# Last chunk pair of the Walsh-Hadamard mix on VectorE, two weight column sums behind the gate stage

## What is computed

```python
def fwht(x):          # normalized Walsh-Hadamard transform over the last dim (1024)
    ...
        x = jnp.stack([a + b, a - b], axis=-2).reshape(-1, n)
def bitlinear(x, w):   return jnp.einsum('bsh,oh->bso', act_quant(x), weight_quant(w))
def h_bitlinear(x, w): return jnp.einsum('bsh,oh->bso', act_quant(fwht(x)), weight_quant(w))
gate = bitlinear(x, w_gate)
up = bitlinear(x, w_up)
intermediate = jax.nn.silu(gate) * up
return h_bitlinear(intermediate, w_down)
```

## Time and profile before

| | |
|---|---|
| runs | 398.34, 399.23, 401.84 us, median 399.23 |
| profiled execution | 401.39 us, its span 399.6 us |
| VectorE busy | 338.6 us (85%) |
| ScalarE busy | 321.7 us (80%) |
| TensorE busy | 309.2 us (77%), weight load 190.9 us (48%) |
| GpSimd busy | 144.3 us (36%) |
| mean granted clock of TensorE | 0.906 of full speed |
| gate stage, from its first matmul to the first Hadamard matmul | 74.6 to 104.8 us |
| from there to the first exponential of the second attention | 104.8 to 159.6 us |

### The profile page before, as it was taken

One profiled execution on the slowest core, in us unless ns is written; L12 is line 12 of the kernel. 1 busy time (PEld: TensorE's weight loads), 2 busy tenths in 40 slices (PEclk: granted clock), 3 DMA queues, 4 the chain that ended last, 5 costly groups with the idle time before them and its releaser, 6 DMA issues.

```text
span 399.6 us, 7596 instructions
## 1 busy us (share of the span) xinstructions
PE 309.2 (77%) x2637; PEld 190.9 (48%) x2637; DVE 338.6 (85%) x556; ACT 321.7 (80%) x523; POOL 144.3 (36%) x315
## 2 busy tenths in 40 slices
PE   6978998777797897558676766877677767789856
PEld 5755555432585885244344443444344444433424
DVE  4665898876889888887899999799999999868996
ACT  3783679974637578899999989899999999977972
POOL 5432345459700322213224555421322132338430
PEclk9996999698699899996999988799999998995687
DMA  8900003600120003768898978789789986900001
GB/s 257 395 3 1 2 7 107 256 1 2 15 90 2 1 2 53 109 129 138 163 177 157 160 135 146 132 145 178 136 160 152 156 147 123 169 2 1 26 28 53
DMA packets 120006, 41.10 MB, mean 103 GB/s; under 512 B 114720, under 2 KB 118432, under 8 KB 119200
## 3 DMA queue, kind: packets, MB, share of 16 engines
q1 hardware_dynamic: 119536, 40.03, 50.7%
q0 software_dynamic: 144, 0.52, 0.3%
q10 hardware_dynamic: 288, 0.07, 0.1%
HBM read 11.24 MB, written 1.05 MB: 31 GB/s over the span
## 4 chain that ended last, share of the span: by engine, by line
PE 26%; ACT 26%; DVE 24%; issue 16%; POOL 6%; DMA 1%; SPq 0%; ACTq 0%; DVEq 0%; POOLq 0%
ACT rb L956 17%; PE ps L1908 4%; DVE nm L1440 4%; PE ps L2003 3%; PE ps L2108 2%; PE ps L1881 2%; PE ps L2015 1%; DVE st L1096 1%; DVE ra L1545 1%; PE ps L2065 1%; DVE small L1547 1%; POOL ra L543 1%; POOL ra L544 1%; DMA xs<-x 1%; PE ps L1780 1%
## 5 line engine op out<-in xcount | busy, mean ns | idle before, releaser
L1440 DVE TENSOR_REDUCE nm<-ps 128x1 f32<-128x1024 f32 x128 | 153.4, 1217 | 15.1 <-PE ps L2003 14.2
L956 ACT ACTIVATE rb<-ps,eb,sq 128x1024 int16<-128x1024 f32 x128 | 153.9, 1219 | 7.9 <-POOL eb L625 7.4
L2003 PE MATMUL ps<-ra,rb 128*128 128x512 bf16 x256 | 83.1, 409 | 46.7 <-ACT rb L956 45.7
L625 POOL TENSOR_SCALAR eb<-nm,sq 128x1 f32<-128x1 f32 x128 | 34.2, 267 | 122.6 <-DVE nm L1440 121.6
L2003 PEld LDWEIGHTS ps<-ra,rb 128*128 128x128 bf16 x256 | 15.9, 100 | 65.6 <-ACT rb L956 62.7
L2030 PEld LDWEIGHTS ps<-ra,tern 128*128 128x128 f16 x624 | 25.3, 97 | 15.5 <-issue 3.8
L956 ACT ACTIVATION_READ_ACCUMULATOR rb<-ps,eb,sq 128x1 f32 x128 | 27.8, 217 | 0.0
L2030 PE MATMUL ps<-ra,tern 128*128 128x16 f16 x624 | 25.8, 170 | 2.0 <-DVE rb L1171 1.4
L1881 PE MATMUL ps<-xqT,tern 128*128 128x512 bf16 x64 | 19.0, 440 | 5.4 <-DVE rb L1349 4.4
L2015 PEld LDWEIGHTS ps<-idh,rb 128*128 128x128 f16 x224 | 15.0, 103 | 14.9 <-issue 8.4
L2015 PE MATMUL ps<-idh,rb 128*128 128x128 f16 x224 | 18.4, 229 | 4.5 <-issue 2.2
(11 more groups left out here) (240 smaller groups left out, 725.6 us busy)
## 6 DMA issues: line engine op xcount, KB each, us to landing
stage<-w SPq DMA_DIRECT2D x2, 1024.0 KB, 6.7
rb<-ra SPq DMA_DIRECT2D x16, 128.0 KB, 2.9
xs<-x SPq DMA_DIRECT2D x4, 256.0 KB, 4.8
cx<-ctx_in SPq DMA_DIRECT2D x4, 256.0 KB, 5.1
stage<-w_gate SPq DMA_DIRECT2D x1, 1024.0 KB, 7.9
stage<-w_up SPq DMA_DIRECT2D x1, 1024.0 KB, 10.6
stage<-w_down SPq DMA_DIRECT2D x1, 1024.0 KB, 4.8
cx<-wide_rows SPq DMA_DIRECT2D x1, 1024.0 KB, 6.7
```

What stands on the lines that cost most here:

```text
L625: nc.gpsimd.tensor_scalar(eb[:, u % 3:u % 3 + 1], nm[:, u % 3:u % 3 + 1], sq[:, t, h:h + 1], LN255, ALU.mult, ALU.add).then_inc(s_bias, 1)
L956: A(esc[u % E_RING], bank(2 * (u % 3), 2), ACT.Exp, bias=eb[:, u % 3:u % 3 + 1], scale=sq[:, t, h:h + 1], accum_out=es[:, t % 2, h:h + 1]) ...
L1440: V.tensor_reduce(nm[:, u % 3:u % 3 + 1], bank(2 * (u % 3), 2), AX.X, ALU.max, negate=True).then_inc(s_max, 1)
L2003: ins = M(bank(2 * (u % 3) + hf), qz[t % 2][:, h // 2, h % 2, :], kT[:, h // 2, 512 * hf:512 * hf + 512], start=True, stop=True)
```

## The change

1. GpSimd no longer does `mix_pair(6)`. VectorE does it in a new function `mix_last_pair`, called in the gate loop behind `gu_product(7)`. It waits for its own product 7 (`gu_out` 8) and for the three other pairs (`mixed_to` 3), and counts `mixed_to` itself.
2. `w_sums(2)` and `w_sums(3)` go from the gate loop of ScalarE to behind the last silu, ahead of `w_round(2)`.
3. On TensorE `w_total(DOWN)` goes behind `hadamard(0)` and `w_total(W1)` behind `hadamard(1)`, the latter now in the bank `D_BANK`; the wait for `g_scaled` ahead of both is gone.
4. On VectorE `w_scales(2)` goes between `mix(0, 0)` and `mix(0, 1)`, and `w_scales(3)` behind `y_scales(1)`; each waits for its own total.
5. In `y_scales` the reciprocal and the rounding factor (which counts `y_scale`) come ahead of `ydq`.

```diff
@@ GpSimd
             mix_four(0, 3)
-            mix_pair(6)
             mix_four(4, 5)
@@ ScalarE
             for n in range(4, 2 * FC):
                 silu(n)
-                if n in (FC + 1, FC + 4):
-                    w_sums(2 + (n - FC) // 3)
...
+            w_sums(2)
+            w_sums(3)
             w_round(2)
@@ VectorE
             def w_scales(i):
-                dve.wait_ge(w_tot, W1 + 1 if i == DOWN else i + 1)
-                b = bank((SUM_BANK, SUM_BANK, T_BANK, T_BANK, Q_BANK)[i])
+                dve.wait_ge(w_tot, i + 1)
+                b = bank((SUM_BANK, SUM_BANK, T_BANK, D_BANK, Q_BANK)[i])
...
+            def mix_last_pair():
+
+                dve.wait_ge(gu_out, FC)
+                dve.wait_ge(mixed_to, 3)
+                V.tensor_tensor(mixed[:, 6, :], inter[:, 0, 6, :], inter[:, 0, 7, :], ALU.add)
+                V.tensor_tensor(mixed[:, 7, :], inter[:, 0, 6, :], inter[:, 0, 7, :], ALU.subtract).then_inc(mixed_to, 1)
...
                     gu_product(n - 2)
+                if n == FC + 1:
+                    mix_last_pair()
...
                 link(V.tensor_scalar(ycl[:, c], ymx[:, c], fac[:, c], EPS, ALU.mult, ALU.max))
-                V.tensor_scalar(ydq[:, c], ycl[:, c], wmean[:, DOWN:DOWN + 1], FP16_UNIT / 128.0, ALU.mult, ALU.mult)
                 link(V.reciprocal(yrc[:, c], ycl[:, c]))
                 V.tensor_scalar(yqs[:, c], yrc[:, c], fac[:, c], 128.0, ALU.mult, ALU.mult).then_inc(y_scale, 1)
+                V.tensor_scalar(ydq[:, c], ycl[:, c], wmean[:, DOWN:DOWN + 1], FP16_UNIT / 128.0, ALU.mult, ALU.mult)
...
+            mix(0, 0)
             w_scales(2)
-            w_scales(3)
-            mix(0, 0)
             mix(0, 1)
             y_scales(0)
             w_clip(2)
             y_scales(1)
+            w_scales(3)
             mix(1, 0)
@@ TensorE
             for n in range(4, 2 * FC):
                 gate_up(n)
-            pe.wait_ge(g_scaled, 2 * FC - 3)
-            w_total(DOWN, bank(T_BANK))
-            w_total(W1, bank(T_BANK))
...
             hadamard(0)
+            w_total(DOWN, bank(T_BANK))
             pe.wait_ge(gu_out, 2 * FC - 1)
             hadamard(1)
+            w_total(W1, bank(D_BANK))
```

## The result

In 22 runs of each, the kernel before had a median of 401.03 us and the changed one of 401.85 us, 0.8 us more. The ratio, from which runs in a slower state of the chip are left out (one of the changed kernel took 443.57 us), is 1.0051 with a 95% interval of 1.0026 to 1.0076: slower by about 2.0 us (1.0 to 3.0). The change costs a little where it was to save. The median lies inside the forecast's range; the shift was forecast as +1.2 us. The forecast's 400.4 us put this shift on 399.23 us, the median of three runs of before; over 22 runs before takes 1.8 us more. A second comparison of the same two kernels gave 1.0016 (0.9987 to 1.0045), that is +0.6 us (-0.5 to +1.8). The profiled execution of the changed kernel has a span of 401.8 us against the 399.6 of the earlier trace rows.

The account below looks back on a forecast made before the run. GpSimd ends the gate stage, with VectorE nearly full behind it. Terms -1.70 + 1.20 + 2.35 + 1.40 - 2.07 = +1.18, called +1.2 us, put on the 399.23 us median: 400.4 us; 8 in 10 between 397.6 and 402.7.

Parts of the forecast that it names:

- the sign: Whole kernel: the change was forecast to make it slower, by +1.2 us.
- a gap before chunk 12: Gate stage: TensorE idles some 3.7 us before chunk 12, waiting for a bank that VectorE frees late.
- slow chunks: Gate stage, TensorE: chunks 12, 13 and part of 14 run at 1.2 GHz after the idle, +1.4 us.
- a first Hadamard product at full clock: Behind the gate stage: TensorE goes from chunk 15 straight into it without idle, 106.1 to 109.55 us.
- the three idles: VectorE behind its first big mix: its waits of 0.83, 0.81 and 0.43 us for TensorE vanish, -2.07 us.
- the covers of the totals: Moved weight totals and scales: ready before VectorE wants them, by 0.5 us (down total) and 1.3 us (second clip).
- Rival 1: VectorE's pair and GpSimd's mix pass each other, no standing and no slow chunks: -2.6 us, 396.7 us; chance 0.12.
- Rival 2: The block happens, but TensorE's clock stays or the slow chunks hide: -0.2 us, 399.0 us; chance 0.20.
- Rival 3: First Hadamard product at lower clock, total behind it, VectorE stands 2.1 us in its mix: +3.3, 402.5 us; chance 0.13.
- the price of the block: Gate loop: VectorE's two-SBUF-input pair stands while GpSimd's mix holds the shared port, +2.35 us, bounds 0 and 4.7.
- the seam: Boundary between GpSimd's two 2.35 us mixes at 95.1 us, where VectorE's pair was expected to ask.
- two waits for the column sums: Gate loop: VectorE's two 0.85 us idles for ScalarE's column sums go when the sums leave the loop, -1.70 us.

Follow-up runs that it names:

- experiment 1: Changed kernel with GpSimd's first mix of four replaced by clearings that only write, so the first half's transform is not computed; ratio to before 0.9907.
- experiment 3: Changed kernel with the last pair back on GpSimd and the old factor order, so only sums, totals and scales are moved; ratio to before 1.0055.
- experiment 12: Changed kernel with the pair three products later, behind product 10 instead of 7; ratio to before 1.0015.
- experiment 8: Changed kernel, unchanged, traced once more; caught at half clock in chunks 8 to 10, pair 0.69 + 2.83 us, end of last big mix +0.46 us.
- experiment 7: Kernel before with only the reciprocal and rounding factor put ahead of the down factor ydq; ratio to before 0.9959.
- experiment 10: Changed kernel, unchanged, timed a second time and traced a third; ratio to before 1.0016, pair 1.83 + 2.82 us.
- experiment 4: Changed kernel with the pair two products later, behind product 9 instead of 7; ratio to before 0.9957.
- experiment 11: Kernel before with the pair on VectorE behind product 9 and the rounding factor ahead of ydq; ratio to before 0.9961.
- experiment 6: Kernel before with only the pair moved, to VectorE behind product 9; ratio to before 0.9902, median 397.67 against 401.51 us.
- experiment 2: Kernel before with only the last pair moved to VectorE, behind product 7; sums, totals, scales and factors as before; ratio to before 1.0019.

## Why the prediction was right, and where it failed

**What held.** That GpSimd and VectorE exclude each other here, that this eats the gain, the sign (by the first comparison and by the stage; the second comparison alone doesn't exclude zero), and the chain behind it: a gap before chunk 12, slow chunks 12 to 14, a first Hadamard product at full clock (3.62 us for 3.45 forecast), the three idles gone, the covers of the totals. Rival 1 (they pass each other) fell with experiment 1, which shows what it would have given. Rival 2 (the clock stays) fell with the row of 4.71 us at a clock of 0.50. Rival 3 didn't happen in the changed kernel, though it did in experiments 3 and 12, as its condition says. By the Trainium skill, "SBUF — State Buffer", section "Who interferes with whom", a VectorE instruction with two SBUF inputs contends with a GpSimd instruction that reads SBUF and not with one that only writes; experiment 1 (0.69 us beside the clearings) and the changed kernel (2.83 us beside the mix) agree with both halves.

**The step that failed** is the size of one term, the price of the block: "+2.35 us ... because both orders at the seam give it". In the changed kernel's profile the distance from product 7 to the next scaling is 5.22 us (92.47 to 97.69) where it was 0.60. Less the pair's own 1.20 that is 3.42 us of standing, not 2.35. The working at the seam was sound: in experiment 8, where they do meet there, 92.03 to 96.10 is 4.07 us, less 0.60 and 1.20 is 2.27. What was wrong was to take the seam as the meeting point, from one execution. With chunks 8 to 10 at full clock, product 7 comes 2.9 us behind GpSimd's third pair instead of 4.2 (92.47 - 89.54 against 94.42 - 90.22), VectorE asks inside GpSimd's first operation, and it waits out the rest of that and then all of the next. The upper bound of 4.7 had been named, but none of the cases stood for what lies between.

**The second step** is from the same source: "-2.07" for the idles behind the first mix. In the full-clock form before idled 2.06 + 0.81 + 0.42 = 3.29 us (experiment 7), since its Hadamard products hang on GpSimd, which doesn't move with the form. These two errors offset each other: +1.07 and -1.46 us. The sum of +1.18 is about twice what the stage came to, so that it lies between the +2.0 and the +0.6 us of the two comparisons is luck and no confirmation of its terms.

**The sum again, from measured terms.** One small correction first: consecutive VectorE operations of 0.68 us start 0.60 apart, so an idle costs about 0.09 us more than the bracket says (the stretch with the bracket of 0.85 is 1.54 us from start to start, 0.94 more than 0.60).

| term, us | forecast | half-clock form | full-clock form |
|---|---|---|---|
| two waits for the column sums | -1.70 | -1.88 | -1.88 |
| pair's two operations | +1.20 | +1.20 | +1.20 |
| standing for GpSimd | +2.35 | +2.27 | +3.42 |
| slow chunks (12 to 14, in experiment 8 13 to 15) | +1.40 | +1.21 | +1.36 |
| idles behind the first big mix | -2.07 | -2.31 | -3.53 |
| sum | +1.18 | +0.49 | +0.57 |
| table above | | +0.46 | +0.58, +0.59 |

The terms were taken from starts: of the changed kernel and experiment 10, of experiment 8, and of before in either form. They close on the table to 0.03 us, and on the comparison of executions of one form, below, to 0.06. The cost in the touched stage is about 0.5 us, and the gain of 2.6 that rival 1 promised is spent on standing (2.3 to 3.4 us) and on the clock (1.2 to 1.4 us), and is there again once the pair is placed where GpSimd is silent.

**A trap.** Measured from product 7, the change costs 1.87 us to the end of the last mix: 36.42 us before (94.42 to 130.84), 38.29 after (92.47 to 130.76). That fits the measured 2.0 us and is nevertheless the wrong reading: it compares a full-clock execution with a half-clock one. Between executions of one form it is 0.55 and 0.63 us.

**What stays open.** The first comparison says +2.0 us (1.0 to 3.0), the second +0.6 (-0.5 to +1.8), the stage +0.5 to +0.6. The medians of the first comparison differ by 0.8 us. The part of its 2.0 us above 0.6 isn't located. Behind the first exponential of the second attention the profiled executions last 239.97, 241.50 and 241.52 us before and 242.47, 241.49 and 241.12 after: no difference stands out of their spread. Experiment 7, whose stage is unchanged, came out at 0.9959 (0.9925 to 0.9993), so a comparison of this length can, it seems, be off by 0.4%, beyond its own interval, and the 0.9957 and 0.9961 of experiments 4 and 11 are no further from 1 than that. Experiment 12 (stage -1.03 us, ratio 1.0015) and experiment 3 (+0.31 us, 1.0055) differ from their stage likewise. The late pair rests on more than one ratio: experiments 4, 6 and 11 agree in sign in both measures (0.9902 to 0.9961, stage -1.69 to -2.63 us). Experiment 6's lead over 4 is not in the stage and isn't claimed. Counted on to the first exponential of the second attention, the distance from the third pair is 69.4 to 69.5 us in the three traces of before, 69.8 to 70.0 in the three of the changed kernel, and 66.6, 66.3 and 66.7 in experiments 4, 6 and 11, one trace each; "pair only" is at 69.2 there, so its +0.79 us in the stage does not last. How often each form occurs was not measured: eight of the traces above show the full clock, six the half.

## What to carry to other kernels

Before work with two SBUF inputs goes from GpSimd to VectorE, look at what GpSimd does at that very moment: if it reads SBUF, VectorE stands, and with two operations in a row it can stand through two of GpSimd's. Place them where GpSimd has to wait for them anyway; here two products later turned +0.5 us in the stage into -1.7 to -2.6. A total that is moved behind a block of matmuls is free only as long as that block starts on time. And where engines meet within a microsecond, take the meeting point from several executions, in the time of the engine that sets the end, not from one trace and not from an engine that is going to wait.

## What the runs showed that was not expected

- The clock in an untouched stretch has two forms: after the same idle of 1.47 us before chunk 8, chunks 8 and 9 took 1.89 us in one execution (89.61, changed kernel) and chunks 8 to 10 4.44 us in another of the same program (87.97, experiment 8). This alone moves product 7 by 1.2 us against GpSimd and decides between 1.83 + 2.83 and 0.69 + 2.83 us.
- Back-to-back GpSimd operations do not lock VectorE out for good: a waiting VectorE instruction gets in at each boundary, and GpSimd's next is then longer by 0.43 to 0.48 us (2.79 and 2.84 against 2.36).
- The clock differs once more further on, here from kernel to kernel. TensorE's Hadamard products for the fifth block took 3.43 us (130.82, changed kernel) after 1.85 us of idle, at a granted clock of 0.58 and 0.57, and 2.05 us (124.20, experiment 6) after 1.72, at 1.00. They took 2.05 us in experiments 2, 3, 6 and 11 and 2.77 to 3.68 us in all ten other traces, among them all three of before and all three of the changed kernel. From the last mix to the first exponential it is 27.8 us in those four and 28.6 to 28.9 in the others; why an edit further ahead decides this was not looked into. It is why the table ends at the last mix.
